# Two layers in one kernel: the last attention sums of layer one in another order, in six banks, with the first unit of layer two's projections put ahead of the second's rows

## What is computed

```python
xn = _layernorm(x, axis=-1)
score = jnp.einsum('blhd,bmhd->bhlm', q, k) / math.sqrt(hd)
ctx = jnp.einsum('bhlm,bmhd->blhd', score, v).reshape(b, l, d)
x = x + ctx @ Wo + bo + moe_top2(xn)           # layer one
xn = _layernorm(x, axis=-1)
x = x + block_attention(xn) + moe_by_capacity(xn)   # layer two, blocks of 64 rows
```

## Time and profile before

| | |
|---|---|
| median of three runs | 725.49 us (724.77 to 725.72) |
| the profiled execution | 724.52 us |
| its span, first to last instruction | 722.8 us |
| PE busy | 683.0 us, 94% |
| DVE busy | 551.6 us, 76% |
| ACT busy | 453.8 us, 63% |
| POOL busy | 447.5 us, 62% |
| mean granted clock of TensorE | 0.997 |

### The profile page before, as it was taken

One profiled execution on the slowest core, in us unless ns is written; L12 is line 12 of the kernel. 1 busy time (PEld: TensorE's weight loads), 2 busy tenths in 40 slices (PEclk: granted clock), 3 DMA queues, 4 the chain that ended last, 5 costly groups with the idle time before them and its releaser, 6 DMA issues.

```text
span 722.8 us, 19559 instructions
## 1 busy us (share of the span) xinstructions
PE 683.0 (94%) x6424; PEld 617.7 (85%) x6424; DVE 551.6 (76%) x1306; ACT 453.8 (63%) x956; POOL 447.5 (62%) x530
## 2 busy tenths in 40 slices
PE   5999998899999999999988999899999999999994
PEld 4898877899999999999967999767678788888894
DVE  5999778978888778886668887599987586666652
ACT  6565457677776777876515888567677774444421
POOL 4577779999996997998322224034454746666363
PEclk9999999999999999999999999999999999999998
DMA  9699874345355544443078986245568666666252
GB/s 246 178 264 298 244 168 107 92 114 139 108 139 164 139 122 133 120 110 109 25 225 258 318 276 190 72 95 131 117 127 214 216 205 147 152 159 157 32 56 32
DMA packets 146118, 112.04 MB, mean 155 GB/s; under 512 B 58337, under 2 KB 136292, under 8 KB 146024
## 3 DMA queue, kind: packets, MB, share of 16 engines
q1 hardware_dynamic: 132696, 84.84, 42.8%
q0 software_dynamic: 12624, 25.35, 14.1%
q10 hardware_dynamic: 704, 0.66, 0.5%
HBM read 66.58 MB, written 40.94 MB: 149 GB/s over the span
## 4 chain that ended last, share of the span: by engine, by line
PE 65%; POOL 13%; DVE 9%; issue 6%; DMA 4%; ACT 2%; SPq 0%; POOLq 0%; ACTq 0%; DVEq 0%
PE banks L1019 13%; PE bank L983 11%; PE bank L1312 11%; POOL rows_by_expert L2471 7%; PE banks L1359 6%; PE bank L1075 6%; PE banks L910 4%; PE banks L1092 3%; DMA rows_by_expert<-rw,slots 2%; PE bank L994 2%; PE bank L966 2%; PE bank L1159 2%; POOL r L2508 1%; PE bank L1332 1%; DVE rw L2165 1%
## 5 line engine op out<-in xcount | busy, mean ns | idle before, releaser
L1019 PE MATMUL banks<-r_split,rt_split 128*128 x852 | 110.9, 284 | 4.2 <-issue 3.6
L1019 PEld LDWEIGHTS banks<-r_split,rt_split 128*128 128x128 f32 x852 | 105.1, 190 | 6.0 <-issue 6.0
L983 PE MATMUL bank<-wq_high_or_w_low_split,rt_split 128*128 128x256 f32 x640 | 99.3, 286 | 2.4 <-DVE rt_split L2004 2.2
L2522 POOL DMA_INDIRECT ults_by_choice_and_token<-rw,y_id x71 | 80.1, 1128 | 34.3 <-ACT rw L1547 22.6
L983 PEld LDWEIGHTS bank<-wq_high_or_w_low_split,rt_split 128*128 128x128 f32 x640 | 86.9, 189 | 4.0 <-DVE rt_split L2004 3.9
L2471 POOL DMA_INDIRECT rows_by_expert<-rw,slots x64 | 66.1, 1033 | 32.2 <-issue 16.0
L2643 POOL DMA_INDIRECT out_x<-r,idx x32 | 50.2, 1569 | 50.1 <-DVE r L2347 42.3
L1312 PE MATMUL bank<-r_split 128*128 128x512 f32 x336 | 78.7, 392 | 0.2 <-DVE r_split L2325 0.2
L2029 DVE TENSOR_TENSOR rt_split<-rw,rt_split 128x512 fp32r<-128x512 f32 x71 | 70.7, 1031 | 9.6 <-ACT rt_split L1540 9.3
L2004 DVE TENSOR_TENSOR rt_split<-r,rt_split 128x512 fp32r<-128x512 f32 x64 | 62.3, 1013 | 19.5 <-ACT rt_split L1467 19.1
L1312 PEld LDWEIGHTS bank<-r_split 128*128 128x128 f32 x336 | 62.5, 188 | 13.0 <-issue 0.4
(11 more groups left out here) (312 smaller groups left out, 1845.3 us busy)
## 6 DMA issues: line engine op xcount, KB each, us to landing
rt<-in_w SPq DMA_DIRECT2D x24, 512.0 KB, 4.7
r<-in_w SPq DMA_DIRECT2D x16, 512.0 KB, 12.4
rw<-rows_by_expert SPq DMA_DIRECT2D x32, 256.0 KB
rt<-ults_by_choice_and_token SPq DMA_DIRECT2D x32, 256.0 KB, 4.0
rw<-in_x SPq DMA_DIRECT2D x16, 256.0 KB
rw<-x_layer SPq DMA_DIRECT2D x16, 256.0 KB, 3.2
x_plus_bias<-rw SPq DMA_DIRECT2D x16, 256.0 KB, 3.2
rows_layer<-rt SPq DMA_DIRECT2D x16, 256.0 KB, 2.8
```

What stands on the lines that cost most here:

```text
L983: last = pe.matmul(bank[1 + b][:, k * 2 * P:(k + 1) * 2 * P], w[:, c, o:o + P], x[d % 2][:, c, :], start=n == 0, stop=n == 3 * DC - 1)
L1019: last = pe.matmul(bank[6 + t % 2][:, 0:D], hidden_T(h, t, c), w[:, ds(e2, 1), o + c * D:o + (c + 1) * D], start=n == 0, stop=n == 3 * HC - 1)
L2522: pool.indirect_dma_start(y0_d[:, :], bass.IndirectOffsetOnAxis(y_id[:, t:t + 1].bitcast(I32), 0), c_y[:, t % XB, :], None, bounds_check=l ...
```

## The change

Four things:

- The sixteen products take turns in six banks (4, 5, 6, 7, 3, 2), so that product k waits for sum k-6; product 2, the first in bank 6, waits until layer one's last results are out of it.
- The bias of the values (one product, two matmuls) goes to bank 1 in place of bank 7, without that wait.
- On PE, unit 0's transposes come behind product 15; then queries and keys of unit 0 (as soon as banks 2 and 3 are read, sum 11), then unit 1's transposes, then values and scores of unit 0. From unit 2 on all is as before.
- On DVE, both combines of unit 0 and its moments come together behind sum 8, and `low_xT(0)`, before behind sum 15, stands between the two combines of unit 1, behind sum 12.

```diff
--- before.py
+++ after.py
@@ -369,6 +369,15 @@
 
         ALL_ROWS = [max(loads(t)[1] for t in range(ST0) if loads(t)[0] == i) for i in range(XB)]
 
+        AO_BANKS = (4, 5, 6, 7, 3, 2)
+        AS = len(AO_BANKS)
+
+        def ao_place(i):
+
+            if i < NE:
+                return bank[4 + i % 2][:, 0:D]
+            return bank[AO_BANKS[(i - NE) % AS]][:, 0:D]
+
         def x_tile(i):
             if i < NE:
                 return q_x[:, i % 4, :, :]
@@ -904,10 +913,14 @@
                 pe.wait_ge(qrot, i + 1)
                 if i == 0:
                     pe.wait_ge(m_sb, NB)
-                if i >= 2:
+                if 2 <= i < NE:
                     pe.wait_ge(ao_sb, i - 1)
+                elif i >= NE:
+                    pe.wait_ge(ao_sb, max(NE, i - AS + 1))
+                if i == NE + 2:
+                    pe.wait_ge(y_sb, ST0)
                 for r in range(DC):
-                    last = pe.matmul(bank[4 + i % 2][:, 0:D], xT_all[:, r, i * P:(i + 1) * P], m_all[:, i // BT, r, :],
+                    last = pe.matmul(ao_place(i), xT_all[:, r, i * P:(i + 1) * P], m_all[:, i // BT, r, :],
                                      start=r == 0, stop=r == DC - 1)
                 last.then_inc(ao_ps, 1)
 
@@ -1047,9 +1060,8 @@
             def bias_of_values():
 
                 pe.wait_ge(wq1_r, 3)
-                pe.wait_ge(y_sb, ST0)
                 for c in range(DC):
-                    last = pe.matmul(bank[7][:, 0:D], bv1_b[:, c, :], wo1_s[:, c, :], start=c == 0, stop=c == DC - 1)
+                    last = pe.matmul(bank[1][:, 0:D], bv1_b[:, c, :], wo1_s[:, c, :], start=c == 0, stop=c == DC - 1)
                 last.then_inc(bo1_ps, 1)
 
             def transpose_unit(v):
@@ -1102,9 +1114,13 @@
                 attend(i)
                 if i == NE:
                     bias_of_values()
-                elif i == NT - 3:
-                    transpose_unit(Unit(0, 0, 2))
-            for u in (1, 2, 3):
+            transpose_unit(Unit(0, 0, 2))
+            pe.wait_ge(ao_sb, NE + 2 * AS)
+            queries_keys(Unit(0, 0, 2))
+            pe.wait_ge(bo1_ps, 2)
+            transpose_unit(Unit(0, 1, 2))
+            values_scores(Unit(0, 0, 2))
+            for u in (2, 3):
                 transpose_unit(Unit(u // 2, u % 2, 2))
                 project_before(Unit(u // 2, u % 2, 2))
             with pe.Fori(2, NU // 2 - 1) as m:
@@ -2033,7 +2049,7 @@
             def add_attention(i):
                 dve.wait_ge(ao_ps, i + 1)
                 dve.wait_ge(xq_r, i + 1)
-                dve.tensor_tensor(x_tile(i), bank[4 + i % 2][:, 0:D].rearrange("p (c n) -> p c n", c=DC), x_tile(i),
+                dve.tensor_tensor(x_tile(i), ao_place(i).rearrange("p (c n) -> p c n", c=DC), x_tile(i),
                                   ALU.add).then_inc(ao_sb, 1)
 
             dve.drain().then_inc(table_r, 1)
@@ -2116,16 +2132,22 @@
                 add_attention(i)
                 if i == NE + 1:
                     dve.wait_ge(bo1_ps, 1)
-                    dve.tensor_tensor(bo1_s[:, :], bo1_s[:, :], bank[7][:, 0:D], ALU.add).then_inc(bo1_ps, 1)
-                elif i in (NE + 8, NE + 9):
-                    combine(0, i - NE - 8)
-                elif i in (NE + 10, NE + 13):
-                    moments_unit((i - NE) // 13)
-                elif i in (NE + 11, NE + 14):
-                    scale_unit((i - NE) // 14)
-                if i in (NE + 11, NE + 12):
-                    combine(1, i - NE - 11)
-            for u in range(NU + 1):
+                    dve.tensor_tensor(bo1_s[:, :], bo1_s[:, :], bank[1][:, 0:D], ALU.add).then_inc(bo1_ps, 1)
+                elif i == NE + 8:
+                    combine(0, 0)
+                    combine(0, 1)
+                    moments_unit(0)
+                elif i == NE + 9:
+                    scale_unit(0)
+                elif i == NE + 11:
+                    combine(1, 0)
+                elif i == NE + 12:
+                    low_xT(0)
+                    combine(1, 1)
+                    moments_unit(1)
+                elif i == NE + 13:
+                    scale_unit(1)
+            for u in range(2, NU + 1):
                 if 2 <= u < NU:
                     combine(u, 0)
                     combine(u, 1)
```

## The result

| | before | changed |
|---|---|---|
| median of 20 runs | 725.49 us (721.88 to 727.61) | 727.31 us (723.53 to 730.22) |
| ratio to before | | 1.0028, 95% interval 1.0017 to 1.0040 |
| profiled execution, its span | 724.52, 722.8 us | 727.21, 725.4 us |
| mean granted clock | 0.997 | 0.994 |

The change costs about 2.0 us (1.2 to 2.9 by the interval). That is inside the range on record. By the ratio it is slower by more than 0.2%, which had a chance of 0.36, and not "no change", which had 0.59; the interval's lower end, 0.17%, lies just under that line.

A forecast was written before the change was run, and what follows sets the result against it. Bound: TensorE, from unit 3's transposes on; their start hangs on VectorE's last sum and SyncE's queue. Queue +1.0 and transfer +0.1 shift it by 1.1, carried to the end: median 725.49 to 726.6, range 725.2 to 728.2.

The forecast's parts named there:

- What bounds the seam: First product to unit 3's transposes (395.06 before): last sum and SyncE's queue set that end; everything behind keeps its length.
- Products through at 379.5, unit 0's transposes there: TensorE: no waits left, sixteen products end at 379.5 instead of about 383.0; unit 0's transposes follow, as before (379.51).
- Sum 15, +1.12: VectorE's last attention sum starts at 384.14, 1.12 us later, because low_xT(0) and its wait stand ahead.
- SyncE, +1.0, bounds 0.6 and 1.4: Store queue ahead of unit 3's load: next issue +1.0 us, +0.1 for the transfer; middle +1.1, bounds +0.6 and +1.4.
- VectorE idle about 2.3 us ahead of combine(3): VectorE waiting for unit 3's expert results: its wait of about 1 us becomes 2.3.
- Unit 2's transposes at 390.35, 25.56 behind the first product: TensorE: unit 2's transposes come at 390.35 instead of 389.63, held by normal(2) waiting for unit 0's store.
- The collision named there: GpSimd's bias sum (388.24) against VectorE's L2105 (388.04): if GpSimd came first, unit 1's projections end at 396.1, still inside 396.2.
- The gap of 3.3 us ahead of unit 2: TensorE's waits for banks and units gather into one idle gap, 387.0 to 390.35, about 3.3 us.
- rival 2: TensorE's clock falls in the new gap, slowing unit 1's projections: +0.5 to +4.2 on top of 1.1, middle 728.9; chance 0.07.
- a clock below 1.00 between 387 and 396: Listed sign of being wrong: TensorE's granted clock below 1.00 between 387 and 396, around unit 1's projections.
- The sum: Whole kernel: the shift of 1.1 carried to the end; span 723.9, profiled time 725.6, median 726.6, counted as no change.
- rival 1: Last store and unit 3's landing are dearer: from +1.45 up to +2.4, 727 to 727.9; chance 0.29.

The follow-up runs named there:

- y3_first: Changed kernel with unit 0's two stores and unit 3's load ahead of the last four of SyncE's sixteen stores; 725.07 us, ratio 0.9994 to before.
- late_sums: y3_fill with three matmuls in the gap, VectorE's sums 14 and 15 behind combine(2), their stores behind unit 1's; 722.92 us, ratio 0.9956 to before.
- late_nofill: late_sums without the three matmuls in the gap; 724.82 us, ratio 0.9991 to before.
- y3_fill: y3_first with four matmuls that nothing reads in the gap ahead of unit 2's transposes; 726.76 us, ratio 1.0008 to before.
- banks_only: Kernel before with the six banks and the bias in bank 1, both engines' orders as before; 725.61 us, ratio 1.0007 to before.

## Why the prediction came out as it did

- *What bounds the seam.* Right that the loss is a shift of unit 3's transposes, wrong that all behind them keeps its length: 0.45 us of the shift came back in unit 3, where a wait of its queries went. The busy share in the earlier trace rows (54.79 of 54.94) hid that wait.
- *Products through at 379.5, unit 0's transposes there.* Right (379.96, with a first product 0.49 later).
- *Sum 15, +1.12.* Right. It came at 384.56 (the second of the two at 384.21), 19.28 us behind the first product against 18.23: +1.05.
- *SyncE, +1.0, bounds 0.6 and 1.4.* +0.84; the last store took 0.62, the median, and started as soon as the one before it was issued. I had added 0.1 for the transfer; unit 3's results reached combine(3) 0.04 sooner relative to the issue. Middle +1.1 measured as +0.8.
- *VectorE idle about 2.3 us ahead of combine(3).* 0.98: the results came a little sooner, and VectorE later, since L2121 took 1.18 us instead of the 0.28 for the whole way reckoned with.
- *Unit 2's transposes at 390.35, 25.56 behind the first product.* 25.64. The collision named there took place, in the other order than reckoned: GpSimd's sum began 0.10 us ahead of L2121, which took 1.18 us. The store of unit 0, which I had as the bound, landed at 389.44 (issued at 386.54, 2.9 us); ScalarE could start only at 389.77, so the collision cost the branch 0.2 to 0.3. Without it the gap would have been about 3.0 us (an estimate from these times), and with the store out of the way too it was 2.24 (y3_first).
- *The gap of 3.3 us ahead of unit 2.* 3.27. The gap was foreseen and its weight wrong: **the step that failed is that the sum puts the clock's fall at nothing, with rival 2's chance at 0.07**, "by the rows nothing of this length was seen inside the work". That no row showed a gap of such a length was taken as evidence that it would be harmless; it was no evidence at all. The clock fell in both profiles, and "a clock below 1.00 between 387 and 396" stands in the prediction's own list of signs of being wrong. By it unit 1's projections, reckoned to end at 395.8, ended at about 397.6 (397.1 with the first product where it was before) and came to decide over unit 3's landing. In the seam that cost 0.7 to 1.4 us; the price on record, +0.5 to +4.2, holds that at its lower end, and the 728.9 in its middle was too much. The Trainium skill (TensorE: Matmul & The Clock Gate, Part 1) has an idle array drop to the halved clock. Here the trace agrees, with 0.50 behind a wait of 3.26 us. That waits of 1.99 and 2.24 us were followed by it too is what these runs show.
- *The sum.* With the seam as measured the sum is +1.46 to +2.07, less the 0.45 that unit 3 gives back +1.0 to +1.6, and the median would have been forecast at 726.5 to 727.1. It was 727.31, 1.8 us above the median before; the interval of the ratio, 1.2 to 2.9 us, holds all but the lower end of that.
- *Luck.* The forecast alone, 726.0 to 727.0, missed the median. The range held it because it had been drawn wide for rival 1, a dearer last link, at 727 to 727.9. But that link wasn't dear: the store took 0.62 us and the last transfer of unit 3 3.6 us (its reckoning had 1.04 and 4.4 to 4.7). A queue cheaper than forecast and a fall of the clock that the sum had put at nothing added up to a number inside the range, which is luck.

## What to carry to other kernels

Gathering small waits of TensorE into one longer wait is not neutral: see what the longest wait is afterwards, and give it work or split it. Two costs that lie over each other have to go together, since curing one alone gives little. Where engine lists are in order, ask of each instruction that is put ahead of another what stands behind that one in the next queue; here the last of sixteen sums released SyncE for a load of another unit, and putting that load ahead of four stores gave 0.4 to 1.0 us back. Two edits of an order may need each other, so that undoing one alone measures neither. And a shift should be measured where the pace has become the same again, not at the first point that is late.

## What the runs showed of the hardware

- Waits of TensorE of 1.99 us (with one of 1.6 ahead of it), 2.24, 3.23 to 3.26 (four times) and 3.90 us were followed by a stretch of 3.41 us at half clock; waits of 1.5 to 1.7 us, alone or two of them 5.6 us apart, were not. One stretch, of 6.82 us, came in late_sums at 465.67 without any wait of over 0.8 us near it, and late_nofill had a wait of 3.34 us at 150.9 with no fall behind it. So a long wait is neither needed nor always enough, and what else decides is open.
- One stretch of 3.41 us at half clock, with TensorE busy throughout and nothing else late, cost 1.55 us (y3_first against y3_fill).
- L2121, an instruction of 128x2 elements on VectorE with both inputs in SBUF, took 1.18 us in all four profiles in which GpSimd's sum had begun 0.10 to 0.12 us ahead of it, and 0.16 where that sum was past or within 0.1 us of its end.
- The time that SyncE takes to issue one and the same transfer was 0.5 to 0.6 us mostly, but 1.04 for the last store in both profiles of the kernel before and 2.26 for the first part of unit 3's load in banks_only. That of the last store repeated with the kernel (1.036 both times); its cause wasn't found.
